# Column tiles of 32 for all attention matmuls, and two head groups in one bank of outputs

## The chip, the cores and the metric

One core of a Trainium2 chip runs the whole kernel. The metric is the device time of one execution in microseconds (us). TensorE does matmuls (PE in the profile, its weight loads PEld), VectorE is DVE, ScalarE is ACT, GpSimd is POOL, and SyncE (SP) issues most transfers.

## The reference, cut to what matters

One transformer block over x of shape (8, 512, 128), in float32: attention with 16 heads of 8 channels, then a mixture of 8 experts of which each token takes 2, plus one expert shared by all.

```python
# B, S, HIDDEN, HEADS, HEAD_DIM = 8, 512, 128, 16, 8
h = layernorm(x)
q, k, v = (h @ W.T + b for W, b in ((Wq, bq), (Wk, bk), (Wv, bv)))   # each split into 16 heads
attn = softmax(q @ k.T / sqrt(8)) * head_mask                        # per sequence and head, 512 x 512
x = x + (attn @ v).reshape(b, s, 128) @ Wo.T + bo
y = layernorm(x)
x = x + gelu(y @ Wfc_s + bfc_s) @ Wproj_s + bproj_s \
      + sum over the top two of 8 experts e: gate[e] * (gelu(y @ Wfc[e] + bfc[e]) @ Wproj[e] + bproj[e])
```

## The kernel before, in words

There are four stages. First LayerNorm, the projections to q, k and v and the splitting of q and k into three bf16 parts each, stored to HBM scratch and loaded back as stacked operands q_op and k_op. Then the attention, then the routed experts over tiles of 128 tokens, then the combination. The change lies in the attention, and its lines in the other stages only set constants or load weights.

The attention walks over 8 sequences (b), in each over 4 head groups (hg) of 4 heads (j), in each over 16 steps s, step s being key tile i = s // 4 and head j = s % 4. Each engine has its own program in this order, and counting semaphores join them. `sequences` unrolls the loop over b in Python.

- `row_scores` (L1154) gives scores with query rows on the partitions, for the maxima alone. It runs two head groups ahead, in four banks of PSUM from BK_A, and ROW_TILES says after which step: one after step 0 of each four, two after step 1, one after step 2, none after step 3. VectorE's `row_max` (L827) takes the maxima of two banks at a time; a group has 8 such pairs p.
- `max_split` on GpSimd splits the maxima into two bf16 parts, `max_rows` (L1198) transposes them on TensorE at step 7 (MX_STEP), `max_out` on ScalarE copies them out, and SyncE writes them as two more rows of q_op (`load_shift`, L313), so that the next group's key scores come out with their row's maximum already subtracted.
- `key_scores` (L1172) gives scores with keys on the partitions, in two banks from BK_S. ScalarE takes the exponential (L676) into probs. Step n may write its bank when the exponential of step n - 2 has ended.
- `pv` (L1183) multiplies the probabilities of four heads with v_op, whose first column is ones, so that row 0 of each head's 32 output rows is the sum. It is one call for each key tile, three steps behind the last exponential that it needs (PV_LAG). The four heads are four column tiles of 32, each in float32 and so two passes, 8 matmuls a call.
- `out_norm` on VectorE, once per group in four steps behind pairs 3 to 6 of the next group: a transposition by 32 x 32 blocks out of PSUM (L835), the reciprocal of the sums (L838), the multiplication with the head mask (L843), and after the last group a second transposition to o_sb (L850).
- Small work of the sequence before is laid between: in group 1 `project_out` (L1209) at steps 0 to 3, `residual` (L858) at pair 1 and `ln2_stats` (L865) at pair 3 on VectorE; then `ln2_scales` on GpSimd (ten small operations, L472 to L486); `ln2_normalise` (L644) on ScalarE at steps -1, 3, 7 and 11 of group 2; `transpose_y` (L1222) at step 13 of group 2, `copy_yT` (L653) at step 15, `router` (L1228) at step 1 of group 3, `router_step` on VectorE at pairs 1, 2, 4 and 5, and `ranks` (L1239 to L1246) at step 14, with `count_step` and `slot_step` at pairs 6 and 7. All of these results of TensorE go through one bank, BK_M, with those of `max_rows`. GpSimd writes the routed rows with indirect transfers (L514).

## Time and profile before

| | us |
|---|---|
| median of three runs | 700.1 (699.42 to 701.23) |
| the profiled execution | 700.0 |
| its span in the trace | 698.2 |
| TensorE busy (weight loads apart) | 633.9 |
| VectorE busy | 540.3 |
| ScalarE busy | 437.9 |
| GpSimd busy | 256.6 |

The largest groups of instructions are L827 on VectorE (256 of them, 304.0 us), L676 on ScalarE (512, 278.8 us), and on TensorE L1154 (512, 181.5 us), L1172 (512, 179.0 us) and L1183 (1024, 136.0 us). Matmuls overlap, since each shows its whole way through the array, so the distance of two starts tells what one costs, not its length. Some matmul records are missing (470 of the 512 of L1172 are there). A number of TensorE's clock in the views, 1.00, is its full level of 2.4 GHz; it is granted through nearly the whole attention. In the timeline's rows "x8" merges neighbours of one line, and the length is that of the whole.

### The profile page before, as it was taken

Reading aid. Unit: us, or ns where it says so; the run is one execution under the profiler, and the core shown is the slowest. Engines: PE = TensorE matmul, PEld = TensorE weight load, DVE = VectorE, ACT = ScalarE, POOL = GpSimd, SP = SyncE. Lnnn points to the kernel's source line nnn. Section 1 sums busy time; section 2 is a strip of 40 time slices with the busy share of each in tenths; the row PEclk is TensorE's granted clock in tenths of the full one; section 3 lists DMA queues with packets and bytes.
Section 4 is the critical chain, followed back from the end, with each engine's and each line's share of the span. In section 5 each row is a group of like instructions: output and inputs, shape, how many; then the busy total and the mean of one; then the engine's idle time right before and its main releaser. Section 6 shows DMA issues by size and latency. Waiting matters only on the chain.

```text
span 698.2 us, 13370 instructions
## 1 busy us (share of the span) xinstructions
PE 633.9 (91%) x3934; PEld 324.6 (46%) x3976; DVE 540.3 (77%) x1180; ACT 437.9 (63%) x953; POOL 256.6 (37%) x386
## 2 busy tenths in 40 slices
PE   1766799999999999999999999997979999999996
PEld 1441222323323323323332332323779999998965
DVE  6998778888998998988989989822656666666558
ACT  0881467777687787787787787793425555555541
POOL 6766200020430420421521512506464555454541
PEclk9996799999999999999999999999999999999998
DMA  5399594411311212212221121000112222212174
GB/s 151 93 335 349 126 237 107 115 46 36 92 44 43 83 43 68 69 45 63 63 64 48 58 69 48 21 1 31 47 50 66 66 65 63 68 59 62 47 246 127
DMA packets 67611, 61.28 MB, mean 88 GB/s; under 512 B 16250, under 2 KB 58106, under 8 KB 67562
## 3 DMA queue, kind: packets, MB, share of 16 engines
q1 hardware_dynamic: 63242, 51.79, 26.7%
q0 software_dynamic: 4320, 8.89, 3.8%
q8 instruction: 25, 0.41, 0.3%
q14 instruction: 24, 0.20, 0.1%
HBM read 35.76 MB, written 24.62 MB: 86 GB/s over the span
## 4 chain that ended last, share of the span: by engine, by line
PE 63%; DVE 14%; issue 7%; SPq 5%; POOL 4%; ACT 4%; DMA 3%; DVEq 0%; ACTq 0%; POOLq 0%; another core or an unknown queue 0%
PE ps L1183 13%; PE ps L1172 13%; PE ps L1154 12%; PE ps L1357 10%; PE ps L1369 8%; DVE mx L827 6%; POOL slots L514 2%; DVE x_sb L1097 2%; SPq L295 2%; DMA q_op<-mxT 2%; PE ps L1309 1%; DVE o_t L835 1%; PE ps L1209 1%; PE ps L1317 1%; SPq L305 1%
## 5 line engine op out<-in xcount | busy, mean ns | idle before, releaser
L676 ACT ACTIVATE probs<-ps 128x512 f32<-128x512 f32 x512 | 278.8, 595 | 102.5 <-PE ps L1172 87.8
L827 DVE TENSOR_REDUCE mx<-ps 128x2 f32<-128x1024 f32 x256 | 304.0, 1212 | 42.8 <-PE ps L1154 37.5
L1154 PE MATMUL ps<-k_op,q_op 96*128 96x512 bf16 x512 | 181.5, 394 | 19.2 <-DVE mx L827 7.0
L1172 PE MATMUL ps<-q_op,k_op 128*128 128x512 bf16 x470 | 179.0, 387 | 2.2 <-DMA q_op<-mxT 1.5
L1172 PEld LDWEIGHTS ps<-q_op,k_op 128*128 128x128 bf16 x512 | 49.6, 98 | 187.5 <-ACT probs L676 127.7
L1183 PE MATMUL ps<-probs,v_op 128*32 128x512 f32 x1024 | 136.0, 604 | 0.5 <-issue 0.2
L723 ACT ACTIVATE probs<-ps,b_cur 128x128 f32<-128x128 f32 x284 | 81.4, 368 | 75.7 <-PE ps L1357 65.3
L577 POOL DMA_INDIRECT results<-rest,row_id x71 | 73.9, 1041 | 75.1 <-DVE rest L1041 57.1
L514 POOL DMA_INDIRECT slots<-route_sb,slot_u x64 | 67.0, 1046 | 75.1 <-ACT probs L676 50.8
L1357 PE MATMUL ps<-xn,qk 128*128 128x128 f32 x568 | 79.2, 284 | 3.7 <-DVE xn L1034 1.7
L1154 PEld LDWEIGHTS ps<-k_op,q_op 96*128 96x128 bf16 x512 | 49.5, 99 | 61.7 <-DVE mx L827 27.6
L1369 PE MATMUL ps<-k_op,probs 128*128 128x128 f32 x568 | 75.3, 276 | 0.0
L1357 PEld LDWEIGHTS ps<-xn,qk 128*128 128x128 f32 x568 | 70.1, 195 | 8.7 <-ACT probs L723 8.3
L499 POOL CAST mx_parts<-mx 128x16 bf16<-128x16 f32 x32 | 6.3, 198 | 184.0 <-DVE mx L827 184.0
L1369 PEld LDWEIGHTS ps<-k_op,probs 128*128 128x128 f32 x568 | 69.3, 192 | 0.2 <-issue 0.2
L1041 DVE TENSOR_TENSOR rest<-ps,b_sb 128x128 f32<-128x128 f32 x71 | 20.2, 285 | 23.9 <-PE ps L1369 23.8
L1034 DVE COPY xn<-ps 128x128 f32<-128x128 f32 x71 | 20.6, 291 | 22.1 <-PE ps L1347 12.8
L1183 PEld LDWEIGHTS ps<-probs,v_op 128*32 128x32 f32 x1024 | 20.4, 108 | 34.8 <-issue 31.2
L702 ACT ACTIVATE probs<-ps,b_sb 128x512 f32<-128x512 f32 x32 | 21.1, 689 | 20.9 <-PE ps L1309 18.4
L1317 PEld LDWEIGHTS ps<-w_sb,probs 128*128 128x128 f32 x256 | 29.5, 192 | 2.1 <-issue 1.9
L1025 DVE COPY qk<-w_sb 128x512 f32 x71 | 29.8, 420 | 0.6 <-issue 0.6
L1317 PE MATMUL ps<-w_sb,probs 128*128 128x128 f32 x256 | 29.9, 276 | 0.0
(135 smaller groups left out, 591.8 us busy)
## 6 DMA issues: line engine op xcount, KB each, us to landing
q_op<-q_scr SPq DMA_DIRECT2D x96, 96.0 KB
k_op<-k_scr SPq DMA_DIRECT2D x96, 96.0 KB
w_sb<-in_W SPq DMA_DIRECT2D x18, 256.0 KB, 4.0
probs<-slots SPq DMA_DIRECT2D x71, 64.5 KB, 1.9
k_scr<-probs SPq DMA_DIRECT2D x16, 256.0 KB, 3.7
q_scr<-probs SPq DMA_DIRECT2D x8, 384.0 KB, 3.1
k_scr<-probs SPq DMA_DIRECT2D x8, 384.0 KB, 3.6
k_scr<-probs SPq DMA_DIRECT2D x16, 128.0 KB, 3.1
```

Of the source, the lines that this page charges most:

```text
L514: nc.gpsimd.indirect_dma_start(slots, bass.IndirectOffsetOnAxis(slot_u[:, K2 * i + k:K2 * i + k + 1], 0), y2[:, i, k, :], None).then_inc(s ...
L577: nc.gpsimd.indirect_dma_start(results, bass.IndirectOffsetOnAxis(row_id[:, v, h:h + 1], 0), r_tile[:, v, h, :], None).then_inc(s_res[v], 16)
L676: nc.scalar.activation(probs[:, i, j, :], ps[:, BK_S + j % key_banks(b, hg), :], ACT.Exp, scale=float(D) ** -0.5).then_inc(s_exp, 1)
L723: nc.scalar.activation(hid_tile[:, par, c, :], ps[:, BK_TU + 2 * par + c // 2, TR * (c % 2):TR * (c % 2 + 1)], ACT.Gelu_apprx_tanh, bias=b ...
L827: nc.vector.reduce_max(mx[:, slot % 2, 2 * p:2 * p + 2], ps[:, bank:bank + 2, :], AX.X).then_inc(s_max, 1)
L1025: nc.vector.tensor_copy(w1_cur[:, v, :], w1_sb[:, e, :])
L1154: last = nc.tensor.matmul(ps[:, BK_A + a % 4, :], q_op[hg][0:SH, j, P * i:P * (i + 1)], k_op[hg][0:SH, j, :], start=True, stop=True)
L1172: nc.tensor.matmul(ps[:, BK_S + j % key_banks(b, hg), :], k_op[hg][:, j, P * i:P * (i + 1)], q_op[hg][:, j, :], start=True, stop=True).the ...
L1183: last = nc.tensor.matmul(ps[32 * j:32 * j + 32, BK_O, :], v_op[:, hg, i, j, :], probs[:, i, j, :], start=(i == 0), stop=(i == NT - 1))
L1317: last = nc.tensor.matmul(ps[:, DN0 + b % 2, C * i:C * (i + 1)], hid[:, b % 2, c, P * i:P * (i + 1)], w2_sb[:, E, c, :], start=(c == 0), s ...
L1357: last = nc.tensor.matmul(ps[:, BK_TU + 2 * par + c // 2, TR * (c % 2):TR * (c % 2 + 1)], w1_cur[:, v, P * c:P * (c + 1)], yT_tile[:, par, ...
L1369: last = nc.tensor.matmul(ps[:, BK_TD + par, C * h:C * (h + 1)], hid_tile[:, par, c, P * h:P * (h + 1)], w2_cur[v][:, c, :], start=(c == 0 ...
```

## The change

All matmuls of `row_scores`, `key_scores` and `project_out` are issued as four with 32 weight columns each, one for each quarter of the output partitions (QUARTERS); the transposition in `max_rows` becomes a matmul with 32 weight columns. `transpose_y`, `router` and `ranks` stay 128 wide.

Two head groups share one bank of outputs: v_op holds an even group's channels in columns 0 to 8 and an odd group's in 16 to 24, and the pv calls of both groups accumulate into the same 32 rows per head (the other columns of v_op are zero). `out_norm` runs once per pair of groups, in groups 2 and 0, and its multiplication no longer takes the mask: GpSimd multiplies Wo's rows with it once, at the start.

Moved: the residual goes from VectorE to GpSimd behind a new copy on ScalarE (`copy_projection`, group 1, step 5), `ln2_stats` from pair 3 to pair 6, `ln2_normalise` to steps 3, 6, 9 and 12, `transpose_y` to step 14, `copy_yT` with it to step 16 (group 3, step 0), `router` from step 1 to step 3, its VectorE steps to pairs 2 to 5, the addition of counts from VectorE to GpSimd (`count_rows`). The last sequence's residual stays on VectorE.

```diff
@@ -232,8 +234,10 @@
-PV_LAG, MX_STEP, YT_STEP = 11, 7, 13
-Y_STEPS = (-1, 3, 7, 11)
+PV_LAG, MX_STEP, YT_STEP = 11, 7, 14
+Y_STEPS = (3, 6, 9, 12)
+AP_STEP = -11
+ROUTER_STEP, ROUTER_PAIRS = 3, (2, 3, 4, 5)
@@ -247,7 +251,9 @@
 L2 = 9
-N_PAD = 6
+N_PAD = 5 + HG
+HALF_OUT = 16
+QUARTERS = [slice(32 * c, 32 * c + 32) for c in range(P // 32)]
@@ -449,7 +452,8 @@
     ln1_rstd(3)
-    nc.gpsimd.memset(v_op[:, :, :, :, 0:1], 1.0).then_inc(s_pad, 1)
+    for hg in range(HG):
+        nc.gpsimd.memset(v_op[:, hg, :, :, HALF_OUT * (hg % 2):HALF_OUT * (hg % 2) + 1], 1.0).then_inc(s_pad, 1)
@@ -461,7 +465,7 @@
         src = v_all[:, b, :, J * D * hg:J * D * (hg + 1)].rearrange("p n (j d) -> p n j d", j=J)
-        nc.gpsimd.tensor_copy(v_op[:, hg, :, :, 1:1 + D], src).then_inc(s_vop, 1)
+        nc.gpsimd.tensor_copy(v_op[:, hg, :, :, HALF_OUT * (hg % 2) + 1:HALF_OUT * (hg % 2) + 1 + D], src).then_inc(s_vop, 1)
@@ -505,6 +509,20 @@
+    def residual(b):
+        if b == 0:
+            pool.wait_ge(s_xbo, B)
+        pool.wait_ge(s_apc, b + 1)
+        sl = x_sb[:, b * NT:(b + 1) * NT, :]
+        nc.gpsimd.tensor_tensor(sl, sl, projected[:, :].rearrange("p (n c) -> p n c", c=C), ALU.add).then_inc(s_x2, 1)
+    def count_rows(b):
+        pool.wait_ge(s_cn, (b + 1) * Q + 1)
+        pool.wait_ge(s_rk, b + 1)
+        nc.gpsimd.tensor_tensor(run_bf[:, :], run_bf[:, :], seq_n[:, :], ALU.add).then_inc(s_cn, 1)
@@ -518,6 +536,9 @@
+    pool.wait_ge(s_wo, 16 * J)
+    pool.wait_ge(s_w, 16 * N_W)
+    nc.gpsimd.tensor_scalar(wo_sb[:, :], wo_sb[:, :], mask_sb[:, 0:1], None, ALU.mult).then_inc(s_wom, 1)
@@ -541,11 +562,13 @@
                 max_split(g + 2)
+            if n == NC - 1 and b > 0:
+                residual(b - 1)
...
                 route_step(b, n)
+        gather_v(b, 3)
...
             ln2_scales(b - 1)
-        gather_v(b, 3)
@@ -555,6 +578,7 @@
             keep_yT(b - 1)
+            count_rows(b - 1)
@@ -652,6 +676,12 @@
+    def copy_projection(b):
+        act.wait_ge(s_ap, b + 1)
+        wait(act, s_x2, b)
+        nc.scalar.activation(projected[:, :], ps[:, BK_M, :], ACT.Copy).then_inc(s_apc, 1)
@@ -682,6 +712,8 @@
                     step = (hg - 2) * J * NT + i * J + j
+                    if step == AP_STEP and not first:
+                        copy_projection(b - 1)
@@ -826,35 +858,34 @@
-    def out_norm(b, hg, step):
-        g = b * HG + hg
+    def out_norm(b, pair, step):
+        n = b * (HG // 2) + pair
+        both = o_t[:, :, :].rearrange("p a (h c) -> p a h c", h=2)
         if step == 0:
-            wait(dve, s_onrm, g)
-            dve.wait_ge(s_pv, (g + 1) * NT)
+            wait(dve, s_onrm, n)
+            dve.wait_ge(s_pv, (n + 1) * 2 * NT)
...
         elif step == 1:
-            dve.wait_ge(s_ot, g + 1)
-            nc.vector.reciprocal(o_rec[:, :], o_t[:, :, 0]).then_inc(s_orec, 1)
+            dve.wait_ge(s_ot, n + 1)
+            nc.vector.reciprocal(o_rec[:, :, :], both[:, :, :, 0]).then_inc(s_orec, 1)
         elif step == 2:
-            dve.wait_ge(s_orec, g + 1)
-            if hg == 0:
+            dve.wait_ge(s_orec, n + 1)
+            if pair == 0:
                 wait(dve, s_o, b)
-            nc.vector.scalar_tensor_tensor(out=o_all[:, :, hg, :], in0=o_t[:, :, 1:1 + D],
-                                           scalar=mask_sb[:, hg:hg + 1],
-                                           in1=o_rec[:, :].unsqueeze(2).to_broadcast([P, S // 32, D]),
-                                           op0=ALU.mult, op1=ALU.mult).then_inc(s_onrm, 1)
-        elif hg == HG - 1:
-            dve.wait_ge(s_onrm, g + 1)
+            nc.vector.tensor_tensor(o_all[:, :, 2 * pair:2 * pair + 2, :], both[:, :, :, 1:1 + D],
+                                    o_rec[:, :, :].unsqueeze(3).to_broadcast([P, S // 32, 2, D]),
+                                    ALU.mult).then_inc(s_onrm, 1)
+        elif pair == 1:
+            dve.wait_ge(s_onrm, n + 1)
...
-        if isinstance(b, int) and b == 0:
-            dve.wait_ge(s_xbo, B)
+        dve.wait_ge(s_xbo, B)
         dve.wait_ge(s_ap, b + 1)
-        sl = x_sb[:, bass.ds(b * NT, NT), :]
+        sl = x_sb[:, b * NT:(b + 1) * NT, :]
@@ -933,28 +965,25 @@
                     row_max(g + 2, p, hg)
-                if 3 <= p < 7 and hg > 0:
-                    out_norm(b, hg - 1, p - 3)
-                elif 3 <= p < 7 and not first:
-                    out_norm(b - 1, HG - 1, p - 3)
+                if 3 <= p < 7 and hg == 2:
+                    out_norm(b, 0, p - 3)
+                elif 3 <= p < 7 and hg == 0 and not first:
+                    out_norm(b - 1, 1, p - 3)
...
                     if hg == 1:
-                        if p == 1:
-                            residual(b - 1)
-                        if p == 3:
+                        if p == 6:
...
                     if hg == 3:
-                        if p in (1, 2, 4, 5):
-                            router_step(b - 1, (1, 2, 4, 5).index(p))
+                        if p in ROUTER_PAIRS:
+                            router_step(b - 1, ROUTER_PAIRS.index(p))
...
                             slot_step(b - 1, 0)
-                            count_step(b - 1, 1)
...
     for step in range(4):
-        out_norm(B - 1, HG - 1, step)
+        out_norm(B - 1, 1, step)
@@ -1151,8 +1180,9 @@
             wait(pe, s_max, (b * HG + hg) * (J * NT // 2) + a // 2 - 1)
-        last = nc.tensor.matmul(ps[:, BK_A + a % 4, :], q_op[hg][0:SH, j, P * i:P * (i + 1)], k_op[hg][0:SH, j, :],
-                                start=True, stop=True)
+        for c in QUARTERS:
+            last = nc.tensor.matmul(ps[c, BK_A + a % 4, :], q_op[hg][0:SH, j, P * i + c.start:P * i + c.stop],
+                                    k_op[hg][0:SH, j, :], start=True, stop=True)
@@ -1169,19 +1199,23 @@
             pe.wait_ge(s_max, NG * (J * NT // 2))
-        nc.tensor.matmul(ps[:, BK_S + j % key_banks(b, hg), :], k_op[hg][:, j, P * i:P * (i + 1)], q_op[hg][:, j, :],
-                         start=True, stop=True).then_inc(s_sb, 1)
+        for c in QUARTERS:
+            last = nc.tensor.matmul(ps[c, BK_S + j % key_banks(b, hg), :],
+                                    k_op[hg][:, j, P * i + c.start:P * i + c.stop], q_op[hg][:, j, :],
+                                    start=True, stop=True)
+        last.then_inc(s_sb, 1)
...
         if i == 0:
-            wait(pe, s_ot, g)
+            if hg % 2 == 0:
+                wait(pe, s_ot, g // 2)
...
             last = nc.tensor.matmul(ps[32 * j:32 * j + 32, BK_O, :], v_op[:, hg, i, j, :], probs[:, i, j, :],
-                                    start=(i == 0), stop=(i == NT - 1))
+                                    start=(hg % 2 == 0 and i == 0), stop=(hg % 2 == 1 and i == NT - 1))
@@ -1190,24 +1224,26 @@
         if hg == 2:
-            wait(pe, s_x2, b)
+            wait(pe, s_apc, b)
...
             pe.wait_ge(s_cn, b * Q)
-        nc.tensor.transpose(ps[:, BK_M, 0:P // 2].bitcast(bf16), mx_parts[:, :], id_bf[:, :]).then_inc(s_mxTp, 1)
+        nc.tensor.matmul(ps[0:SHIFTS * J * NT, BK_M, 0:P], mx_parts[:, 0:SHIFTS * J * NT], id_bf[:, :],
+                         start=True, stop=True).then_inc(s_mxTp, 1)
...
         if i == 0:
-            pe.wait_ge(s_wo, 16 * J)
+            pe.wait_ge(s_wom, 1)
...
                 pe.wait_ge(s_cn, (b + 1) * Q)
-        last = nc.tensor.matmul(ps[:, BK_M, C * i:C * (i + 1)], o_sb[:, P * i:P * (i + 1)], wo_sb[:, :],
-                                start=True, stop=True)
+        for c in QUARTERS:
+            last = nc.tensor.matmul(ps[c, BK_M, C * i:C * (i + 1)], o_sb[:, P * i + c.start:P * i + c.stop], wo_sb[:, :],
+                                    start=True, stop=True)
@@ -1285,7 +1321,7 @@
                         transpose_y(b - 1)
-                    if hg == 3 and s == 1:
+                    if hg == 3 and s == ROUTER_STEP:
```

## Rows read from the trace of the kernel before

**Rows 1.** The page, section 1: busy us, share of the span, instructions
```profile
PE 633.9 (91%) x3934; PEld 324.6 (46%) x3976; DVE 540.3 (77%) x1180; ACT 437.9 (63%) x953; POOL 256.6 (37%) x386
```

**Rows 2.** Busy time by stretch: one middle sequence, and a dense stretch of three microseconds
```profile
284.25:334.56 50.31, 49.13 (x286) 15.80 (x291) 45.08 (x70) 38.02 (x74) 14.16 (x33) 1.00 0.22 59
...
469.10:472.10 3.00, 3.00 (x34) 1.19 (x34) 0.99 (x6) 2.61 (x6) 0.38 (x1) 1.00 0.00 0
```

**Rows 3.** The timeline (start us, us, ...) of TensorE matmuls over one plain block
```profile
301.27 0.39 PE L1172 MATMUL ps<-q_op,k_op 128*128 128x512 bf16 x1
...
301.49 0.38 PE L1154 MATMUL ps<-k_op,q_op 96*128 96x512 bf16 x1
...
302.40 0.39 PE L1172 MATMUL ps<-q_op,k_op 128*128 128x512 bf16 x1
...
302.89 0.39 PE L1172 MATMUL ps<-q_op,k_op 128*128 128x512 bf16 x1
303.21 1.07 PE L1183 MATMUL ps<-probs,v_op 128*32 128x512 f32 x8
304.21 0.39 PE L1172 MATMUL ps<-q_op,k_op 128*128 128x512 bf16 x1
```

**Rows 4.** ScalarE: the timeline of the same stretch, then a group by shape
```profile
299.94 1.08 ACT L676 ACTIVATE probs<-ps 128x512 f32<-128x512 f32 x2 [0.36 <-PE ps L1172]
...
301.75 2.16 ACT L676 ACTIVATE probs<-ps 128x512 f32<-128x512 f32 x4 [0.24 <-PE ps L1172]
...
L653 ACT ACTIVATE xnT<-ps 128x512 f32<-128x512 f32 x8 | 4.8, 602 | 0.7 <-PE ps L1222 0.7
```

**Rows 5.** The timeline of TensorE at the end of the attention
```profile
469.82 0.19 PE L1239 MATMUL ps<-chosen,tri_bf 128*128 128x64 bf16 x1
...
470.09 0.38 PE L1172 MATMUL ps<-q_op,k_op 128*128 128x512 bf16 x1
...
470.39 2.78 PE L1183 MATMUL ps<-probs,v_op 128*32 128x512 f32 x24
```

**Rows 6.** Groups by shape: TensorE's weight loads
```profile
L1172 PEld LDWEIGHTS ps<-q_op,k_op 128*128 128x128 bf16 x512 | 49.6, 98 | 187.5 <-ACT probs L676 127.7 <-issue 36.7 <-DVE tab_e L923 3.4
...
L1183 PEld LDWEIGHTS ps<-probs,v_op 128*32 128x32 f32 x1024 | 20.4, 108 | 34.8 <-issue 31.2 <-ACT probs L676 3.6
```

**Rows 7.** VectorE: groups by shape, then the timeline of a plain block
```profile
L827 DVE TENSOR_REDUCE mx<-ps 128x2 f32<-128x1024 f32 x256 | 304.0, 1212 | 42.8 <-PE ps L1154 37.5 <-issue 4.9
...
L835 DVE STREAM_TRANSPOSE o_t<-ps 128x512 f32<-128x512 f32 x32 | 22.6, 707 | 9.0 <-PE ps L1183 9.0
...
L843 DVE SCALAR_TENSOR_TENSOR o_all<-o_t,mask_sb,o_rec 128x128 f32<-128x128 f32 x32 | 10.8, 339 | 0.1
...
L865 DVE BATCH_NORM_STATS2 stats<-x_sb 128x6 f32<-128x128 f32 x32 | 6.7, 270 | 0.2 <-DVE x_sb L858 0.2
...
302.35 2.36 DVE L827 TENSOR_REDUCE mx<-ps 128x2 f32<-128x1024 f32 x2 [0.59 <-PE ps L1154]
```

**Rows 8.** The timeline: TensorE's small work of one sequence
```profile
288.63 0.38 PE L1209 MATMUL ps<-wo_sb,o_sb 128*128 128x128 f32 x2
...
311.25 0.60 PE L1222 MATMUL ps<-id_sb,route_sb 128*128 128x128 f32 x4
...
314.53 0.95 PE L1228 MATMUL ps<-wr_sb,xnT 128*128 128x8 f32 x8
```

**Rows 9.** GpSimd: LayerNorm's scalars in the timeline, first and last; a group by shape
```profile
296.96 0.20 POOL L472 TENSOR_TENSOR mean_d<-stats 128x4 f32<-128x4 f32 x1 [1.00 <-DVE stats L865]
...
300.11 0.20 POOL L486 TENSOR_TENSOR neg_shift<-neg_mean,rstd 128x4 f32<-128x4 f32 x1
...
L525 POOL TENSOR_TENSOR x_sb<-x_sb,bo_sb 128x512 f32 x8 | 9.8, 1261 | 0.0
```

**Rows 10.** The timeline: matmuls that waited, for VectorE and for a transfer
```profile
299.29 0.39 PE L1154 MATMUL ps<-k_op,q_op 96*128 96x512 bf16 x1 [0.24 <-DVE mx L827]
...
88.93 0.39 PE L1172 MATMUL ps<-q_op,k_op 128*128 128x512 bf16 x1 [0.56 <-DMA q_op<-mxT]
```

20 lines of the change are left out of this document (10 added, 10 removed).

## The prediction

> **What bounds the kernel now.** I read the page's busy time first, then one sequence in the windows view, then the timeline inside it. On the page TensorE is busy 91% and VectorE 77% of the span [rows 1]. Attention has eight sequences, and the six middle ones repeat each other in 50.31 us. In one of them TensorE is busy 49.1 us, VectorE 45.1, ScalarE 38.0 [rows 2], so TensorE is first, but VectorE has only 5 us free, and a gain on TensorE meets it soon.
>
> A sequence is 4 groups of 4 blocks. I write K for a key_scores matmul, R for a row_scores matmul; a block is K R K R R K R K and then one pv call. The reader should follow one plain block [rows 3]: K1 at 301.27, R 0.22 us later, K4 at 302.89 (1.62 after K1), PV 0.32 after K4, the next K1 1.00 after PV: 2.94 in all. Three things in it are not streaming. (1) PV starts 0.32 after K4 where an R starts 0.22 after a K: 0.10. (2) PV to the next K1 takes 1.00. The end of the attention has three pv calls in a row, 24 matmuls in 2.78 us, and one call alone, 8 in 1.07 [rows 3, 5]; so four more rounds of four quarters took 1.71, or 0.43 each, and two rounds are 0.86. The missing 0.14 is the way out of the 32-column mode. (3) K4 is late: seven matmuls at 0.22 would bring it at 1.53. It waits for the second exponential: the first starts 0.48 after K1 (301.75), two take 1.08 [rows 4], so they end at 1.56, and K4 starts at 1.62.
>
> **The plain block after.** Each K and R becomes four quarter matmuls, so K, R and PV all run in column tiles of 32. No row shows this with bf16; the nearest is the PV stream, whose rounds cost 0.43 each, with each load hidden beneath the matmuls [rows 5]. Half of that is what one bf16 matmul takes today, 0.22, so I take 0.22 per round. The bounds: not below 0.22 (the same columns stream), and not above 0.22 plus one whole exposed load, 0.11 [rows 6]. K4 then comes at 1.65 (the exponentials, plus 0.02 because the last quarter starts that much later), PV 0.24 after it (a round, and 0.02 for loads that could not run ahead of a waiting K), the next K1 0.86 later: 2.75. That is 0.197 less than 2.945, and 16 blocks give -3.15 us per sequence.
>
> The Trainium skill (TensorEngine Tiling, Restrictions) says that column tiling switches fast weight load off, which speaks against this change. Today's full loads take 98 ns and the quarters' 108 [rows 6]; they lie beneath matmuls of 216 ns, so row and rule together still leave 0.22; if the rule meant exposed loads, it would be the last rival below.
>
> **What is moved, per middle sequence.**
> - project_out: today two passes 0.11 apart per tile (the second starts 0.27 before the pair's end, 0.38) [rows 8]; after, two rounds of about 0.115 each. The way out of PV before the fourth one goes. About -0.1.
> - transpose_y, router and ranks stay 128 wide, so each now enters and leaves the full mode: 0.10 twice. transpose_y is the same 4 matmuls [rows 8] and loses 0.21. The router's 8 passes at 0.11 [rows 8] today lie between R and K, where they fill the wait for the exponentials; at step 3 they come behind PV, where nothing waits: +0.40. Ranks (0.27 from its start to the next K [rows 5]) sit before a waiting K4 as today; switch and hidden wait about cancel: 0.
> - VectorE. In a block two reduce_max take 2.36 and 0.59 is idle before them [rows 7]; a shorter block leaves 0.40 to 0.46. Out_norm's transposition (0.71) and reciprocal go from four to two per sequence, the multiplication takes both groups (0.34 for 128 elements [rows 7], about 0.42 for 256), the residual leaves: about 2.5 us less. But pieces longer than the slack still stop R at the next pair: a lateness of about 0.17 is free, and another 0.12 is hidden because K4 waits for ScalarE. The transposition with reciprocal (0.63 and 0.18 net of overlap) costs about 0.25 in group 0 and 0.10 in group 2, the bn_stats (0.75 for four of 0.27, overlapped [rows 7]) now follow pair 6 alone and cost 0.45, the router's max_index 0.25: 1.05. Today's stops of that kind are two per sequence; at 299.29 the row records the last 0.24 of one [rows 10], and I put both together at 0.65, an estimate from it. So +0.40. The bounds are 0 (all hidden) and twice 1.05.
> - ScalarE copies the projection (0.60, as its copy of yT [rows 4]) after step 5 of group 1. max_rows of step 7 must wait for it, since both use bank 7: the copy ends 2.16 after that block's K1, max_rows is due at 1.88: +0.27. The copy costs the exponentials nothing (0.7 us a block is idle).
> - copy_yT moves to step 16, behind the first exponential of group 3's first block. The second exponential then ends 0.50 later, and it is the one that K4 waits for: +0.50. Today it follows the fourth, before idle time.
> - LayerNorm's scalars: bn_stats comes three pairs later, and GpSimd's ten operations take 3.35 us (296.96 to 300.31 [rows 9]). They are ready 3.8 us into group 2, but the first ln2_normalise stands at step 3, where ScalarE arrives at 3.1. It waits 0.7 with the next exponentials queued behind it, and K waits for those: +0.65.
> - residual on GpSimd (1.26 by an addition of its size [rows 9]) ends before pair 6's statistics; count_rows, the quarter memsets and the masking of wo_sb lie beside other work; three fewer mask loads on SP lie ahead of waits for data. Nothing for these beyond 0.2 at the start; were GpSimd's cover gone, the residual would put its 1.3 on the LayerNorm chain.
>
> Sum: -3.15 - 0.1 + 0.21 + 0.40 + 0.40 + 0.27 + 0.50 + 0.65 = -0.82 us per sequence.
>
> **The whole.** Six middle sequences: -4.9. In the first, groups 1 and 2 begin when a transfer lands (K at 88.93 waited 0.56 us for q_op<-mxT [rows 10]) and SP's queue sets that time, so what is saved before it is lost; eight blocks save 1.6. In the last, two groups have no R and follow ScalarE; eight blocks save 1.6, the waits give back 1.2: -0.4. Start and end +0.4 (wider multiplication, small work). Together -6.5. The profiled execution took 700.0 us (its span 698.2, 1.8 around it), the median of three is 700.1. So 693.5.
>
> **The rivals.**
> - A. The forecast, 693.5 (688 to 699): 0.48.
> - B. The waits that I laid on ScalarE's and GpSimd's moved steps don't show, because TensorE is late there anyway. For it: several meet in one block. Against it: each was worked out from a K with no slack. 1.42 less in six sequences and some in the last: 684. Chance 0.14.
> - C. No change: VectorE gives the gain back. Its idle time per block falls by a third, and if its stops cost twice 1.05, six sequences lose 6.3: 700. Chance 0.16.
> - D. Slower: TensorE's instructions are not supplied fast enough. A block goes from 32 loads and matmuls (8 K and R, 8 of PV, each with its load) to 80. From the point of 2.75/80 = 34 ns per instruction supply decides. A dense stretch of three microseconds of before has 34 matmuls and 34 loads, 44 ns each [rows 2]; a burst of ten small matmuls with their loads runs in 0.27, 14 ns each [rows 5]. Neither proves the limit: the first had nothing more to do, the second may have been queued. Near the middle, at 37 ns, a block takes 2.96, nothing is gained there and the other terms (+2.33) stay: six sequences +14, with the ends 716. At 44 ns it would be over 760. Chance 0.14.
> - E. The rounds take longer than 0.22 because loads are partly exposed. At 0.24 (the round after a mode change shows some 0.02) the time is 699; with half a load, 0.27, a block is 3.04, and the time 727. The PV stream speaks against it. Chance 0.08.
>
> The Trainium skill (TensorE: Matmul & The Clock Gate, "Wait — 56ns, not 53.3ns?") gives about 62 ns per matmul when its sequencer decodes in ucode. By that an estimate for 40 matmuls is 2.5 us, still under a block, and only the blocks with project_out would be held, which gives 697. The burst above ran faster than that, if it was not queued.
>
> **How the numbers follow.** A measurement of this kernel tells about 0.3% from no change, so 698 to 702. Faster: most of A and all of B, 0.60. Same: C, and edges of A and E, 0.17. Slower: D, most of E, the edge of C, 0.23. The range runs from 682 (below B) to 712 (into D).
>
> **What would show it.** In the timeline of the changed kernel: quarter matmuls that start nearly together, in rounds of 0.22; K4 at 1.65; PV 0.24 behind it; the next K1 0.86 behind PV; a plain block of 2.75. A gap before max_rows in group 1 released by ScalarE's copy; ScalarE's first ln2_normalise released by GpSimd; K4 of group 3's first block late by 0.5. The prediction is wrong if rounds are longer than 0.24, if quarters start unevenly with idle named "issue", or if a plain block waits for VectorE's reduce_max.

## The result, and the profile after

The changed kernel takes 711.2 us (median of four, 710.17 to 712.88) against 700.7 us for the kernel before on the same chip: ratio 1.015, 95% interval 1.012 to 1.018. It is slower. The profiled execution took 710.67 us, its span is 708.8.

One fact has to stand ahead of all numbers, since the runs below met it. The chips fall into two kinds. On one, which I call kind A, the kernel before takes 700 us (the first result, e5 to e8, and e9 to e12); on the other, kind B, 690 us (e1 to e4, e13 to e16, and e17 with e18). The changed kernel's ratio is 1.015 to 1.017 on kind A and 1.002 on kind B. The forecast was made from a profile of kind A, and "after" and "before" without more are that first pair. No profile of the kernel before is from kind B.

The profile page's section 1 of after (busy us, share, instructions), then its busy time over one middle sequence, columns as in [rows 2]:

```profile
PE 629.1 (89%) x7240; PEld 343.9 (49%) x7240; DVE 523.7 (74%) x1118; ACT 442.2 (62%) x960; POOL 267.6 (38%) x404
...
285.22:337.22 52.00, 48.59 (x702) 17.82 (x700) 43.03 (x62) 38.60 (x75) 15.72 (x35) 1.00 0.22 58
```

A middle sequence took 50.31 us [rows 2] and takes 52.00, though VectorE has 2 us less to do and TensorE's matmuls cover a little less time: what was added is waiting. A plain block does what was forecast. The timeline of after (the answer to [rows 3]; "x4" are the quarters of one key_scores or row_scores):

```profile
308.02 1.07 PE L1217 MATMUL ps<-probs,v_op 128*32 128x512 f32 x8
308.88 0.43 PE L1203 MATMUL ps<-q_op,k_op 128*32 128x512 bf16 x4
309.09 0.43 PE L1184 MATMUL ps<-k_op,q_op 96*32 96x512 bf16 x4
...
310.57 0.40 PE L1203 MATMUL ps<-q_op,k_op 128*32 128x512 bf16 x4
310.79 0.60 PE L1217 MATMUL ps<-probs,v_op 128*32 128x512 f32 x4
```

K1 stands 0.86 behind pv, R 0.21 behind K1, K4 1.69 behind K1, the next pv 0.22 behind K4: 2.77 in all.

Where the time is, read as the distance from each pv call to the next, 16 to a sequence, worked out from the timelines. The first column is group 0's last block, then come the four of groups 1, 2 and 3, then the first three of the next sequence's group 0. The letters mark what the changed kernel has there: project_out (P), max_rows behind the copy (M), the wait for statistics and for LayerNorm's scalars (L, L), transpose_y (T), copy_yT (C), router and max_rows (X), ranks (N). The runs e2 to e18 are described in the next section; "second" is a run's second sequence, the other rows are a later one.

```
                      P    M              L    L         T    C    X         N
before         2.94 3.56 3.31 2.94 3.26 2.94 3.00 2.94 3.28 3.65 3.00 2.94 3.64 2.94 3.00 2.94  50.31
after (A)      3.56 3.51 3.31 2.77 2.94 3.34 3.37 2.77 3.45 3.21 4.53 2.77 3.62 2.72 2.73 3.39  52.00
e18, after (B) 2.81 3.62 3.31 2.76 2.72 3.30 3.35 2.77 3.45 3.21 4.54 2.77 3.62 2.72 2.73 2.78  50.47
e2, tiles (B)  2.72 3.55 2.94 2.78 3.48 2.72 2.73 2.78 3.41 3.70 2.72 2.79 4.06 2.72 2.73 2.78  48.62
e10, tiles (A) 3.55 3.51 2.94 3.47 2.79 2.72 2.73 2.78 3.41 3.70 2.72 2.79 4.06 2.72 2.73 3.12  49.74
e13, full (B)  2.94 3.56 3.53 2.94 2.95 3.29 3.36 2.96 3.43 3.43 4.46 2.94 3.41 2.94 2.96 2.96  52.06
e6 (A), second 2.82 3.62 2.94 2.78 2.78 2.72 2.73 2.77 3.52 3.70 2.72 2.79 3.61 2.72 2.73 3.46  48.41
e15 (B)        2.82 3.62 2.94 2.78 2.78 2.72 2.73 2.78 3.51 3.21 4.53 2.77 3.62 2.72 2.73 2.78  49.03
e17 (B)        2.82 3.62 2.94 2.78 2.78 2.72 2.73 2.77 3.51 3.21 3.83 2.78 3.63 2.72 2.73 2.78  48.34
```

The 10.6 us between the two profiled spans are made up so: start of the pv calls +1.2, first sequence -4.1 (48.91 to 44.82), second +0.4, five middle ones +8.4, last +1.9, from the last pv calls to the end +2.8. Two things make up the loss. One is waits that the moved work brings; most of these were in the forecast, one was not. The other was in no part of it: matmuls whose end becomes known to the other engines late.

**The wait that was missed.** Timeline of after, the block of 4.53 us:

```profile
321.05 0.40 PE L1203 MATMUL ps<-q_op,k_op 128*32 128x512 bf16 x4
...
321.65 0.18 DVE L903 COPY logits<-ps 128x32 f32<-128x32 f32 x1
...
321.98 0.22 PE L1232 MATMUL ps<-id_bf,mx_parts 128*32 128x128 bf16 x1 [0.53 <-DVE logits L903]
```

`max_rows` of step 7 (L1232) writes the bank in which the router's logits lie, so it must wait until VectorE has copied them. It starts 0.93 behind the key_scores at 321.05, where a round takes 0.22, so 0.71 is the wait. The change moved the router from step 1 to 3 and its copy from pair 1 to 2, right against step 7; I had costed the router's own matmuls only.

**The late starts.** The same place in the third and later sequences, group 0's last block: after on kind A, then the same kernel on kind B (e18).

```profile
284.74 0.96 POOL L532 DMA_INDIRECT slots<-route_sb,slot_u  x1 [1.92 <-ACT probs L706]
...
286.08 0.39 PE L1203 MATMUL ps<-q_op,k_op 128*32 128x512 bf16 x4
...
286.30 0.39 PE L1184 MATMUL ps<-k_op,q_op 96*32 96x512 bf16 x4
...
286.46 0.96 POOL L532 DMA_INDIRECT slots<-route_sb,slot_u  x1 [0.76 <-issue]
...
286.52 0.39 PE L1203 MATMUL ps<-q_op,k_op 128*32 128x512 bf16 x4
...
287.18 2.43 ACT L706 ACTIVATE probs<-ps 128x512 f32<-128x512 f32 x4 [1.00 <-PE ps L1203]
```

```profile
283.16 0.39 PE L1203 MATMUL ps<-q_op,k_op 128*32 128x512 bf16 x4
...
283.40 0.96 POOL L532 DMA_INDIRECT slots<-route_sb,slot_u  x1 [0.63 <-ACT probs L706]
...
283.66 1.08 ACT L706 ACTIVATE probs<-ps 128x512 f32<-128x512 f32 x2 [0.54 <-PE ps L1203]
```

ScalarE begins 0.50 after the key_scores on kind B and 1.10 after it on kind A. TensorE is not slow there: its next matmuls start 0.2 and 0.4 later on both. Only its message is late, and the trace's own record of semaphore updates says so: in after the update that this key_scores makes stands at 287.10, 0.63 behind the matmul's modelled end, and ScalarE starts 0.08 behind the update; in e18 it is 0.03 behind the end. ScalarE's message to TensorE is not held there: the weight load at 286.30 needs the exponential that ended at 286.18. The exponentials then finish late, TensorE waits for them, and that block takes 3.6 or 4.0 instead of 2.8. All such places are in groups 0 and 1 from the third sequence on, while GpSimd issues its eight indirect writes of a sequence (L532); there are none in the first two sequences, which have no writes, and none in groups 2 and 3. From the third sequence on after has 35 exponentials and reduce_max that start more than 0.3 late (0.4 to 1.4), and each time the late update of TensorE's semaphore is recorded 0.5 to 1.6 behind the start of one of these writes. e18 has none. At the end it is at its plainest, because eight writes follow each other (479 to 489 in after, 471 to 481 in e18). First after, then e18:

```profile
483.53 1.08 PE L1245 MATMUL ps<-wo_sb,o_sb 128*32 128x128 f32 x32 [2.56 <-issue]
...
488.38 0.96 POOL L532 DMA_INDIRECT slots<-route_sb,slot_u  x1 [0.31 <-issue]
...
490.99 0.69 DVE L889 TENSOR_TENSOR x_sb<-ps,x_sb 128x512 f32<-128x512 f32 x1 [7.56 <-remote]
491.03 1.28 ACT L734 ACT_TABLE_LOAD   x1 [11.37 <-remote]
```

```profile
475.17 1.08 PE L1245 MATMUL ps<-wo_sb,o_sb 128*32 128x128 f32 x32 [2.56 <-issue]
...
476.38 0.69 DVE L889 TENSOR_TENSOR x_sb<-ps,x_sb 128x512 f32<-128x512 f32 x1 [1.31 <-PE ps L1245]
```

The projection ends at 484.6 in after, and VectorE's residual begins 6.4 us later, 1.65 behind the end of the last write's record; on kind B it begins 0.1 us after the projection. In the other seven runs with tiles that met kind A (e5, e6, e7, e9 to e12) the residual stands 1.5 to 1.7 behind the last write too.

### The profile page after: what moved, and what is told of

It reads as the page before. It is cut to its first block, busy times and chain, and to the rows that moved or that the text cites. A ratio compares the mean times of both kernels' runs of the same rounds, so it can differ in the third digit from the quotient of the medians.

```text
span 708.8 us, 19898 instructions
## 1 busy us (share of the span) xinstructions
PE 629.1 (89%) x7240; PEld 343.9 (49%) x7240; DVE 523.7 (74%) x1118; ACT 442.2 (62%) x960; POOL 267.6 (38%) x404
## 4 chain that ended last, share of the span: by engine, by line
PE 58%; DVE 11%; ACT 9%; issue 7%; POOL 5%; SPq 4%; DMA 3%; another core or an unknown queue 1%; ACTq 0%; DVEq 0%; POOLq 0%
PE ps L1203 12%; PE ps L1393 11%; PE ps L1217 11%; PE ps L1184 10%; PE ps L1405 7%; DVE mx L859 4%; ACT probs L706 4%; DVE x_sb L1126 2%; SPq L298 2%; PE ps L1345 1%; POOL slots L532 1%; DMA k_scr<-probs 1%; POOL rstd L488 1%; ACT probs L755 1%; PE ps L1264 1%
## 5 line engine op out<-in xcount | busy, mean ns | idle before, releaser
L706 ACT ACTIVATE probs<-ps 128x512 f32<-128x512 f32 x512 | 283.1, 596 | 100.0 <-PE ps L1203 94.3
L1203 PE MATMUL ps<-q_op,k_op 128*32 128x512 bf16 x2048 | 201.4, 387 | 16.6 <-ACT probs L706 10.7
L1184 PE MATMUL ps<-k_op,q_op 96*32 96x512 bf16 x2048 | 189.9, 397 | 13.9 <-DVE mx L859 8.0
L1217 PE MATMUL ps<-probs,v_op 128*32 128x512 f32 x1024 | 132.8, 593 | 0.0
L1203 PEld LDWEIGHTS ps<-q_op,k_op 128*32 128x32 bf16 x2048 | 54.8, 95 | 155.8 <-ACT probs L706 108.9
L1184 PEld LDWEIGHTS ps<-k_op,q_op 96*32 96x32 bf16 x2048 | 54.8, 97 | 92.5 <-DVE mx L859 40.0
L532 POOL DMA_INDIRECT slots<-route_sb,slot_u x64 | 66.9, 1046 | 69.4 <-ACT probs L706 47.3
L1217 PEld LDWEIGHTS ps<-probs,v_op 128*32 128x32 f32 x1024 | 31.4, 108 | 8.0 <-issue 0.6
L1345 PE MATMUL ps<-v_all,w_sb 128*128 128x512 f32 x64 | 30.4, 622 | 4.8 <-ACT probs L734 4.8
```

The costliest lines, as they stand in the source:

```text
L532: nc.gpsimd.indirect_dma_start(slots, bass.IndirectOffsetOnAxis(slot_u[:, K2 * i + k:K2 * i + k + 1], 0), y2[:, i, k, :], None).then_inc(s ...
L706: nc.scalar.activation(probs[:, i, j, :], ps[:, BK_S + j % key_banks(b, hg), :], ACT.Exp, scale=float(D) ** -0.5).then_inc(s_exp, 1)
L1184: last = nc.tensor.matmul(ps[c, BK_A + a % 4, :], q_op[hg][0:SH, j, P * i + c.start:P * i + c.stop], k_op[hg][0:SH, j, :], start=True, sto ...
L1203: last = nc.tensor.matmul(ps[c, BK_S + j % key_banks(b, hg), :], k_op[hg][:, j, P * i + c.start:P * i + c.stop], q_op[hg][:, j, :], start= ...
L1217: last = nc.tensor.matmul(ps[32 * j:32 * j + 32, BK_O, :], v_op[:, hg, i, j, :], probs[:, i, j, :], start=(hg % 2 == 0 and i == 0), stop=( ...
L1345: nc.tensor.matmul(ps[:, UP0 + c, :], w1_sb[:, E, P * c:P * (c + 1)], yT[:, b, :], start=True, stop=True).then_inc(s_up, 1)
```

## The experiments

Ratios are to runs of the kernel before on the same chip, with 95% intervals. In the expected texts, theory L says that late starts need column tiles together with the indirect writes, and rival P that they come from the moved work.

**Tiles without the moves, moves without the tiles.** e1_full and e13_full (kind B both) are the changed kernel with

```diff
-        QUARTERS = [slice(32 * c, 32 * c + 32) for c in range(P // 32)]
+        QUARTERS = [slice(0, P)]
```

> The changed kernel with key_scores, row_scores and project_out at full width (QUARTERS is one slice of 128); the shared bank, the moved work and the narrow max_rows stay. In the changed kernel, from the third sequence on, in head groups 0 and 1 only, exponentials and reduce_max start 0.6 to 1.4 us after the matmul they wait for, and at the end the projection's semaphore comes 6 us late. Theory L: this needs column tiles together with GpSimd's indirect writes. Then no late start is left here, plain blocks are 2.94 us, the waits made by the moved work (ln2 scales, copy_yT, router, projection copy) stay at about their size, a middle sequence takes 51.0 to 51.6 us against 50.31 before, and the kernel 704 to 709 us. Rival P: the late starts belong to the moved work, not to the tiles. Then they are here too, a middle sequence takes over 52.5 us, and the kernel 714 us or more.

> The changed kernel with key_scores, row_scores and project_out at full width, as e1_full, for the chip of this call. If before takes 700 us here: theory L (tiles and indirect writes together) expects no late start and middle sequences of 52.05 us as in e1_full, 1.74 more than before, a ratio of 1.017 to 1.022 as on the other chip. Rival P (the moved work makes the late starts) expects middle sequences above 52.7 us and a ratio above 1.025.

Measured 1.020 (1.018 to 1.022) and 1.017 (1.015 to 1.020), 52.06 us per middle sequence in both, no late start. That is more than the 51.0 to 51.6 us expected; e1's 703 us come near the expected 704 only because the chip is of the faster kind. So the moved work and the shared bank, at full width, cost 1.75 us per sequence. Whether they alone would make late starts these two can't tell, since no kernel has them on kind B; what the tiles do alone the next pair tells.

e2_tiles (kind B) and e10_tiles (kind A) are the kernel before with the tiles alone:

```diff
+                for c in QUARTERS:
+                    last = nc.tensor.matmul(ps[c, BK_S + j % key_banks(b, hg), :],
+                                            k_op[hg][:, j, P * i + c.start:P * i + c.stop], q_op[hg][:, j, :],
+                                            start=True, stop=True)
...
-                nc.tensor.transpose(ps[:, BK_M, 0:P // 2].bitcast(bf16), mx_parts[:, :], id_bf[:, :]).then_inc(s_mxTp, 1)
+                nc.tensor.matmul(ps[0:SHIFTS * J * NT, BK_M, 0:P], mx_parts[:, 0:SHIFTS * J * NT], id_bf[:, :],
+                                 start=True, stop=True).then_inc(s_mxTp, 1)
```

> The kernel before with only the column tiles: key_scores, row_scores and project_out as four quarters, max_rows as one tile of 32 columns. No work is moved, each head group keeps its own output bank. Theory L (tiles and indirect writes together make the late starts): plain blocks 2.72 to 2.78 us, late exponentials and reduce_max in groups 0 and 1 from the third sequence on, about 1.2 us per sequence, middle sequences about 49 us, the first 4 us shorter, and 3 to 4 us lost at the end: 690 to 694 us. Rival P (late starts come from the moved work): none here, middle sequences about 47.8 us, nothing lost at the end, 680 to 684 us.

> The kernel before with only the column tiles, as in e2_tiles, to have it on the chip of this call. Where before takes 690 us: 48.62 us per sequence and a ratio of 0.981 again. Where it takes 700 us: late starts in groups 0 and 1 add 0.7 to 1.3 us per sequence and 1 to 4 us at the end, and the ratio is 0.988 to 0.998.

Measured 0.981 (0.979 to 0.983) on B and 0.999 (0.997 to 1.000) on A, with 48.62 and 49.4 to 50.4 us per middle sequence. e2 without a late start seemed to speak for rival P; it was the chip. e10 and the kernel before have the same writes at the same steps; before has no late start in its attention (50.31 in every middle sequence, in both its profiles of kind A; on e10's own chip only its time is known, the same 700.2 us), and e10 has 36. So on kind A the tiles are enough to expose the attention to them; the moved work is not needed.

**The writes.** e4_noputs (kind B) leaves out GpSimd's writes during the attention and takes the routed rows and results from x instead; it does not compute the block, and its profile is read only up to the end of the attention. e3_puts (kind B) and e11_puts (kind A) set the writes closer together:

```diff
-        PUT_STEPS = (2, 5, 8, 11, 14, 17, 20, 23)
+        PUT_STEPS = (2, 4, 6, 8, 10, 12, 14, 17)
```

> The changed kernel with GpSimd's eight indirect writes of a sequence closer together: released after exponentials 2, 4, 6, 8, 10, 12, 14 and 17 of the sequence instead of every third up to 23. Theory L: late starts follow the writes: in group 0 as many or more, in group 1 after its second exponential none. Middle sequences 51.3 to 52.5 us, the kernel 707 to 713 us. Rival S (late starts belong to steps of the schedule, whatever GpSimd does): they stay at steps 3 and 10 of group 1 and pairs 1 of group 1, and the time stays within 1 us of 711.

> The changed kernel without GpSimd's indirect writes during the attention (their semaphore is raised by GpSimd instead); the tiles of the routed experts are then loaded from x and the routed results from x, so only the time up to the end of the attention can be compared. Theory L: no late exponential or reduce_max in any sequence, the sequences from the third on take 50.7 to 50.8 us as the second does in the changed kernel (50.75) instead of 52.0, the last pv call is 6 to 7 us earlier. The last sixteen writes after the attention are kept, so the projection's semaphore is still late there. Rival S: sequences of 52.0 us as in the changed kernel.

> The changed kernel with the eight indirect writes of a sequence released after exponentials 2, 4, ... 14 and 17, as in e3_puts. Where before takes 690 us it tells nothing beside e9 (ratio 1.001 again). Where before takes 700 us: if a start is late when it falls just behind a write, the late ones move to group 0 and are as many or more, sequences 51.0 to 52.5 us; if the late starts come only of the particular steps at which the writes stood, they are gone, 50.46 us, and the ratio falls to 1.003.

e3: 1.001 (0.999 to 1.003), e4: 689.6 us in its one run; they take 50.47 and 50.46 per sequence. I first read this as the theory shown; it was not, because on kind B the unaltered kernel has no late start either (e18). e11 decides: 1.029 (1.026 to 1.031) on kind A, the late starts now in group 0 and costing more, 52.2 to 53.3 per sequence, and group 1's last block clean (2.72). The late starts follow the writes, and packing these makes it worse. A kernel without the writes was not run on kind A.

**The same kernel on both kinds.** e5_after and e9_after met kind A, e18_after kind B.

> The changed kernel again, unaltered, so that it stands beside runs of the same chip. With the writes closer together (e3_puts) no start was late and the ratio to before was 1.001; with the writes gone (e4_noputs) the sequences took the same 50.46 us. Theory L (the writes spread over groups 0 and 1 make the starts late): here the sequences from the third on take 52.0 us, and the ratio to before is 1.012 to 1.018. Rival C (the late starts are a matter of the chip, the runs of e1 to e4 were on another than the first two): no late start, sequences of 50.45 us, ratio 0.999 to 1.003.

> The changed kernel once more, beside e10 to e12 on one chip. So far two kinds of chips were met: on one the kernel before takes 700 us and tiled kernels have late starts in groups 0 and 1 (and the routed tiles of every kernel some 10 us more), on the other it takes 690 us and e1 to e4 had none. Theory: the late starts belong to the chip and to GpSimd's indirect writes. Where before takes 700, this has late starts, middle sequences of 51.1 to 52.1 us and a ratio of 1.012 to 1.020; where it takes 690, none, sequences of 50.46 us and 0.999 to 1.004. The rival (spread writes make late starts on every chip) expects 52.0 us and 1.015 on either.

> The changed kernel, unaltered. Where before takes 690 us: no late starts, 50.46 us per middle sequence as in e3_puts and e16_logits' other blocks, ratio 0.999 to 1.003. Where before takes 700 us: 1.015 to 1.018 as in e5_after and e9_after.

Measured 1.017 (1.014 to 1.021), 1.016 (1.013 to 1.019) and 1.002 (1.000 to 1.003). At the end of the attention, the residual starts 6.4 and 5.6 us after the projection in e5 and e9, 6.3 in e10, 0.13 in e18; with the projection at full width it is 0.04 in before and in e8_before, on kind A too.

> The kernel before again, for a profile on the chip of these runs. Rival C expects middle sequences of 50.31 us as in the first profile, and the difference between chips after the attention; a chip that is slower everywhere would show in every block.

e8 met kind A: 699.2 us, every block as in the first profile. It and e18 also show that kind A costs the kernel before something of its own. VectorE's addition behind a routed tile's last matmul, 71 of them, groups of before, after and e18 (the last figures are idle time ahead and what ended it):

```profile
L1041 DVE TENSOR_TENSOR rest<-ps,b_sb 128x128 f32<-128x128 f32 x71 | 20.2, 285 | 23.9 <-PE ps L1369 23.8
```

```profile
L1070 DVE TENSOR_TENSOR rest<-ps,b_sb 128x128 f32<-128x128 f32 x71 | 20.1, 284 | 23.3 <-PE ps L1405 22.6 <-issue 0.7
```

```profile
L1070 DVE TENSOR_TENSOR rest<-ps,b_sb 128x128 f32<-128x128 f32 x71 | 20.2, 284 | 4.2 <-PE ps L1405 3.7
```

23.9 us of waiting against 4.2, while GpSimd writes each tile's results with the same kind of indirect transfer. Part of it only changes place: the copy at the head of a tile waits less on kind A (before, then e18),

```profile
L1034 DVE COPY xn<-ps 128x128 f32<-128x128 f32 x71 | 20.6, 291 | 22.1 <-PE ps L1347 12.8 <-issue 5.7 <-PE ps L1357 3.2
```

```profile
L1063 DVE COPY xn<-ps 128x128 f32<-128x128 f32 x71 | 20.7, 291 | 31.9 <-PE ps L1383 31.8
```

so that the two waits together are 46.0 against 36.1. From the first to the last of the 71 writes it is 142.8 us in before and 132.7 in e13: these 10 us are the difference between the kinds.

**Two tiles of 64.** e14_halves (kind B) is e6_shared (below) with

```diff
+        QUARTERS = [slice(64 * c, 64 * c + 64) for c in range(P // 64)]
```

> e6_shared with key_scores, row_scores and project_out as two tiles of 64 columns instead of four of 32 (pv stays at 32): 48 matmuls and loads in a block instead of 80. If the mode costs nothing between 64 and 32, plain blocks stay at 2.72 to 2.78 us; if each change of tile size costs as from 128 to 32 (0.10 in, 0.14 out), they are 2.90 to 2.95. Late starts, where before takes 700 us: if they go with the number of TensorE's instructions, they are fewer than e6_shared's one microsecond per sequence or gone; if any column tile makes them, as many. Ratio 0.985 to 1.000.

Measured 1.005 (1.003 to 1.008), plain blocks 2.98 to 2.99, a little over the 2.90 to 2.95 that the same cost of a switch would give: going between 64 and 32 costs at least as much as going between 128 and 32. It met kind B, so what it was to say of the late starts stays open.

**The moved work, piece by piece.** e6_shared (kind A) puts all of it back and keeps tiles and shared bank; e12_best (kind A) is e6 with e3's packed writes; e7_router (kind A) puts back the router's group:

```diff
-        PV_LAG, MX_STEP, YT_STEP = 11, 7, 14
-        Y_STEPS = (3, 6, 9, 12)
-        ROUTER_STEP, ROUTER_PAIRS = 3, (2, 3, 4, 5)
+        PV_LAG, MX_STEP, YT_STEP = 11, 7, 13
+        Y_STEPS = (2, 5, 8, 11)
+        ROUTER_STEP, ROUTER_PAIRS = 1, (1, 2, 4, 5)
```

> The changed kernel with the moved work put back: residual and the update of the counts on VectorE, no projection copy on ScalarE, LayerNorm scalars, copy_yT, transpose_y and the router where they stood before. Column tiles and the shared output bank stay. If the moves cost what the forecast and the block table say (copy before max_rows 0.35, ln2 scales 0.60, copy_yT 0.5, router 1.8 against 0.95 before it), a middle sequence takes 47.6 to 48.2 us and the ratio to before is 0.968 to 0.978, less than with the tiles alone (0.981), because VectorE has two output transpositions less. Rival: the shared bank alone gives nothing, since VectorE's stops only change place: 48.6 us, ratio 0.980 to 0.983.

> The changed kernel with only the router's group of steps put back: the router's matmuls at step 1 of group 3 and VectorE's four pieces after pairs 1, 2, 4 and 5, transpose_y at step 13, the normalisation at steps 2, 5, 8, 11 so that it is ready. Theory: in the changed kernel max_rows of step 7 waits until VectorE has copied the logits out of the bank that both use, and that block takes 4.53 us; here it falls under 3.4, the block of step 0 to 3 gets up to 0.5 longer, and a sequence is 0.8 to 1.5 us shorter: ratio 0.985 to 0.993 times the changed kernel's on the same chip. Rival: the 1.8 us are those of the router's own matmuls and the mode change, then the time stays within 0.3 us per sequence.

> Column tiles and the shared output bank without the moved work (e6_shared), with the indirect writes released as in e11_puts. Where before takes 690 us: sequences of 48.4 us, as e6_shared's second one, against 48.62 with the tiles alone: ratio 0.976 to 0.982. Where it takes 700: between 0.982 and 0.996, below e6_shared's 0.994 if the packed writes make fewer late starts.

e6: 0.994 (0.992 to 0.996), faster than both kernels on kind A, but far from the 0.968 to 0.978 expected, since later sequences have late starts and take 49.3 to 49.6. In its second one only the last block has a late start; with 2.78 there the row sums to 47.73, in the range expected, so beside e2's 48.62 the shared bank is worth 0.9 us. e12: 1.000 (0.998 to 1.002); packed writes take the gain away, as in e11. e7: 1.017 (1.014 to 1.020), no gain where 0.7 to 1.5% was expected: the block of 4.53 fell to 2.72 and the one before it rose from 3.21 to 3.70, but the normalisation, now one step earlier, waited longer for GpSimd's scalars (3.37 to 3.99, the next 2.77 to 3.26). I had changed two things at once. e16_logits (kind B) moves the copy alone, e15_residual (kind B) the residual and statistics alone:

```diff
-        ROUTER_STEP, ROUTER_PAIRS = 3, (2, 3, 4, 5)
+        ROUTER_STEP, ROUTER_PAIRS = 3, (1, 3, 4, 5)
```

> The changed kernel with only one piece of VectorE's work earlier: the copy of the logits out of the bank after pair 1 of group 3 instead of pair 2; the router stays at step 3. Theory: max_rows of step 7 waits for this copy (0.7 us in the trace) and the block of 4.53 us falls to 3.7 to 4.0; a sequence 0.5 to 0.8 us shorter, ratio to the changed kernel about 0.993. Rival: the copy then waits for the router's matmuls with the next reduce_max behind it, row_scores waits for that, and the block stays above 4.3.

```diff
-                            if step == AP_STEP and not first:
-                                copy_projection(b - 1)
...
-                                if p == 6:
+                                if p == 1:
+                                    residual(b - 1)
+                                if p == 3:
                                     ln2_stats(b - 1)
```

> The changed kernel with the residual back on VectorE after pair 1 of group 1, straight from the bank, the statistics after its pair 3, and no copy of the projection on ScalarE; all else as in the changed kernel. The forecast's prices for these steps: 0.27 (max_rows waits for the copy) and 0.65 (ln2_normalise waits for GpSimd's scalars), and part of VectorE's stops comes back. So a middle sequence 0.7 to 1.1 us shorter than the changed kernel's without late starts (50.46): blocks of groups 1's second and 2's first two near 2.95, 2.75 and 2.75 instead of 3.31, 3.30 and 3.33. Rival: the stops of VectorE by residual and statistics take as much as the waits did, under 0.3 us gained.

e16: 0.994 (0.991 to 0.996), the block at 3.83, 0.70 less, the size of the wait. e15: 0.985 (0.982 to 0.987), 49.03 per sequence, 1.43 less, where 0.7 to 1.1 was expected. These rows of after's timeline show what e15 removes, VectorE's stop (row_scores waits for reduce_max behind the statistics) and ScalarE's wait for GpSimd's scalars:

```profile
303.77 0.40 PE L1184 MATMUL ps<-k_op,q_op 96*32 96x512 bf16 x4 [0.56 <-DVE mx L859]
...
305.83 0.20 POOL L490 TENSOR_TENSOR neg_shift<-neg_mean,rstd 128x4 f32<-128x4 f32 x1
...
306.17 0.60 ACT L668 ACTIVATE route_sb<-x_sb,neg_shift,rstd 128x256 f32<-128x256 f32 x1 [0.65 <-POOL neg_shift L490]
```

e17_both (kind B) has both repairs.

> The changed kernel with both repairs: residual and statistics back on VectorE (as e15_residual) and the copy of the logits after pair 1 (as e16_logits). If they add up, middle sequences without late starts take 49.03 - 0.70 = 48.33 us; ratio to before 0.976 to 0.980 where before takes 690 us. Where before takes 700, late starts add about 1.1 us per sequence and 2 to 4 us at the end: ratio 0.990 to 0.997. Rival: with VectorE fuller, the pieces meet in one pair and the second repair gives back half or more.

Measured 0.981 (0.978 to 0.983), 48.34 per sequence: they add up to within 0.01 us. It is no better than the tiles alone (e2, 0.981), but better than either given kernel. e6, whose clean row sums to 0.6 us less per sequence, did not meet kind B and was not tried there.

## Why the prediction was wrong

Two steps failed. The router's term put the wait for its results in the shared bank at nothing, and it is 0.70 us per sequence. And no term had late starts, which cost about 11 us in all. The terms one by one:

- **Plain block 2.75.** Right: 2.72 to 2.78 in all tiled kernels, rounds of 0.21 to 0.22, pv 0.22 behind K4, K1 0.86 behind pv. Alone it is worth 1.69 per middle sequence (e2), not 3.15, because blocks with small work keep their length.
- **Rivals D and E (supply, exposed loads).** Did not happen. Eight quarter matmuls of the projection took one round, 0.22 us, or 27 ns each:

```profile
286.40 0.39 PE L1245 MATMUL ps<-wo_sb,o_sb 128*32 128x128 f32 x8
286.62 0.39 PE L1203 MATMUL ps<-q_op,k_op 128*32 128x512 bf16 x4
```

  That is from e18. The Trainium skill (TensorE: Matmul & The Clock Gate, "Wait — 56ns, not 53.3ns?") gives about 62 ns per matmul with hardware decoding off; the 27 ns here are under half of it, so these runs are not in that state. The Trainium skill (TensorEngine Tiling (Array Packing), Restrictions) says that column tiling disables fast weight load; in after the loads of key_scores with 32 columns take 95 ns, where the full ones took 98, and in rounds of 0.22 no cost of it shows.
- **project_out -0.1.** Wrong by 0.35: its rounds are 0.22 before and after (4 in the block, 0.88; 3.62 is 2.75 and 0.87). Before, 0.3 of them lay where K waited for ScalarE anyway (3.56 is 2.94 and 0.62). The faster block took that cover away.
- **Copy before max_rows +0.27.** Right in mechanism, 0.10 short: 3.31 with it, 2.94 without (e15), 0.37.
- **Statistics, a stop of 0.45, and scalars late, +0.65.** Right in mechanism, nearly in size: 3.30 and 3.35 against 2.72 and 2.73 in e15, 0.58 and 0.62.
- **copy_yT +0.50.** Right: 3.21 is 2.75 and 0.46. **transpose_y**: 3.45 is 0.70 over a plain block, where 0.34 (before) and 0.21 were counted, 0.15 short. **Ranks 0**: 0.87 over a plain block (3.62) against 0.70 before (3.64), 0.17 short.
- **VectorE's other stops, too dear.** For out_norm and the router's max_index 0.60 was counted. In e18 the plain blocks where they could show take 2.73 to 2.81, hardly anything over 2.75, and before's stops at the fifth column (3.26) and its three blocks of 3.00 are gone. This gave back about 0.5.
- **Router +0.40.** The first step that failed. Its matmuls were right (e16's 3.83 is 1.08 over a plain block; 0.71 before and 0.40 make 1.11). The wait of max_rows for VectorE's copy out of the same bank, 0.70 per sequence, was put at nothing, though I had worked out that very wait for the other user of the bank, copy_projection.
- **Middle sequence.** -0.82 was forecast and +0.16 came on kind B. Of the 0.98 between them 0.70 is the logits' wait; project_out, ranks, transpose_y, the statistics and the copy before max_rows were 0.1 to 0.35 short each, 0.9 together, and VectorE's other stops gave most of that back. So the small remainder is partly luck: errors that cancel.
- **First sequence -1.6.** It was -4.1. I had counted eight blocks only, since what is saved ahead of a transfer would be lost. But the waits for that transfer (q_op<-mxT) come and go with the execution: 1.5 us in before (48.91), none in e8_before (47.27), 0.8 in after. So some of the 4.1 is not the change's. Without such a wait it is 47.27 against 43.83 (e4_noputs, whose first sequence is that of the changed kernel): 3.4, sixteen blocks at 0.2. The changed kernel itself took 44.8 to 45.5, and 47.6 in e5.
- **The ends +0.4.** They were +4.0. The pv calls began 1.2 later (85.6 against 84.4). TensorE had been idle, and its granted clock stayed at the 0.50 level, 1.2 GHz, for 3 us more than in before. That is not the main cause: in e9 and e18, the same kernel, it rose at 80.5 and the pv calls still began at 85.4 and 85.3; and in e8_before it rose only at 82.4 and they began at 85.1. All sixteen profiles with tiles begin them at 85.2 to 86.7, the four at full width at 84.1 to 85.1; what in the tiles delays them stays open. The windows of before and after, columns as in [rows 2]:

```profile
80.00:81.00 1.00, 0.85 (x5) 0.31 (x4) 0.55 (x1) 1.00 (x3) 0.00 (x0) 1.00 0.32 66
```

```profile
80.00:81.00 1.00, 1.00 (x16) 0.14 (x8) 1.00 (x2) 0.74 (x2) 0.00 (x0) 0.50 0.31 68
...
82.00:83.00 1.00, 1.00 (x16) 0.44 (x12) 0.71 (x1) 0.46 (x1) 0.00 (x0) 0.50 0.30 66
```

  The tail's 2.8 (230.6 against 227.8 from the three last pv calls on) is mostly the message that came 6 us late: on kind B the tail of after (218.3) is only 0.7 to 1.0 over e1's and e13's.
- **Late starts.** The second step that failed, and the larger: they are in no term and no rival, since the prediction let every engine start as soon as the matmul it waits for has ended. 52.00 less 50.47 is 1.5 per sequence with writes, about 8 us in the middle ones, 1.0 in the last and some 2 in the tail: 11 in all. Nothing in the attention of before showed them, but its routed tiles did, with the 23.9 us ahead of L1041, though only a profile of kind B tells that this wait need not be. I had read the trace only where the change lay.

From 693.5 to 710.7 are 17.2 us: 5.9 in six middle sequences by the missed terms, 7.9 by late starts there, 2.3 in the last sequence, 3.6 at the ends, less 2.5 in the first. With the missed wait alone the answer would have been about 698, and with all the missed terms about 699, what kind B shows, no difference to speak of; on kind A the late starts make it slower. Their mechanism inside the chip stays open.

## What to carry to other kernels

When work that uses a shared bank is moved, write down every reader and writer of the bank in order and cost each hand-over, not only the moved instruction. A faster block takes away the cover of whatever lay in its waits, so multiply a gain only by the blocks that hold nothing else. And change one placement at a time: on one kind of chip the tiles alone gained 1.9%, the moves with the shared bank lost 1.7 to 2.0%, and together they looked like nothing. And when runs come from several chips, put the kernel before beside each of them: the same tiles are worth 1.9% on one kind and 0.1% on the other.

## What the hardware showed

- The same program takes 690 us on some chips and 700 on others. The 10 us lie in the routed tiles, where GpSimd's indirect writes run beside many short matmuls. Where such writes meet the tiled attention on kind A, the updates of TensorE's semaphores come 0.4 to 1.4 us late (up to 1.7 with packed writes, e12), and up to 6.4 us under eight writes in a row, while its matmuls go on.
- In the attention it takes column tiles to bring this out: 40 matmuls and as many loads in 2.75 us, where the full width has 16 and as many in 2.94; the routed tiles, which have it in every kernel, have about 17 and as many in 2.05. So it looks as if the number of TensorE's instructions mattered, but that is only argued: the kernel with halves met a chip without late starts, and the size of the tiles would explain the attention as well. What in the chip delays the signal, and what makes the two kinds, stays open.
- The Trainium skill (Perfetto Trace Analysis, DMA Instruction — SWDGE (GPSIMD)) says that the record of such a transfer shows the making of its descriptors and not the moving of data. The trace agrees: the last write's record in after ends at 489.34, its packets move from 489.92 to 490.26, its semaphore is updated at 490.5, and the held updates of TensorE follow from 490.90 on, just ahead of the residual at 490.99.
- Going from 64 columns to tiles of 32 and back costs at least as much as from 128: plain blocks of 2.98 and 2.94 us, against 2.75 with 32 throughout.
